# A graph attention layer's aggregation: three source tiles in split F32R products, their low parts made by transfers, a ring of five logit buffers

## The reference, cut to what matters

```python
h = (x @ W.T).reshape(n, heads, out_ch)
a_src = jnp.einsum('nhc,hc->nh', h, att_src)
a_dst = jnp.einsum('nhc,hc->nh', h, att_dst)
e = jax.nn.leaky_relu(a_src[src] + a_dst[dst], NEG_SLOPE)
m = jax.ops.segment_max(e, dst, num_segments=n)
ex = jnp.exp(e - m[dst])
denom = jax.ops.segment_sum(ex, dst, num_segments=n)
out = segment_sum(ex / (denom[dst] + EPS) * h[src], dst)   # 8 heads of 128, then + bias, relu
```

## Time and profile before

| what | value |
|---|---|
| median of three runs | 714.68 us (713.36 to 715.59) |
| the profiled execution's own time | 713.25 us |
| its span | 711.4 us |
| TensorE, VectorE, ScalarE, POOL busy | 701.1, 529.0, 420.0, 114.1 us |
| F32 products with PT (L1426) | 161.0 us, 730 records |
| transposes of L (L1402) | 94.2 us, 800 records |
| L2078 and L2087 on VectorE | 117.9 and 113.4 us, 80 each |

### The profile page before, as it was taken

How to read it: one execution, slowest core, us unless ns; L and a number is a source line. 1 busy time by engine, 2 the same in 40 slices (tenths; PEclk the granted TensorE clock), 3 DMA queues, 4 the chain that set the end, 5 groups by cost and what they waited for, 6 DMA issues and landing times.

```text
span 711.4 us, 13502 instructions
## 1 busy us (share of the span) xinstructions
PE 701.1 (99%) x4670; PEld 657.9 (92%) x4670; DVE 529.0 (74%) x878; ACT 420.0 (59%) x863; POOL 114.1 (16%) x95
## 2 busy tenths in 40 slices
PE   8899999999999999999999999999999999999997
PEld 6699999889899999999999999999999899999997
DVE  5999888698899999999999664445568752737232
ACT  4665584388688888888888754454443333522202
POOL 2559421000000000000000000000223331222202
PEclk9999999999999999999999999999999999999999
DMA  8727888645314131322310443201881734315102
GB/s 279 223 68 195 262 244 232 174 140 163 95 40 114 31 102 55 94 67 64 102 32 22 109 111 67 62 0 36 247 282 49 222 91 189 100 58 177 44 23 67
DMA packets 53362, 84.10 MB, mean 118 GB/s; under 512 B 15081, under 2 KB 36399, under 8 KB 53312
## 3 DMA queue, kind: packets, MB, share of 16 engines
q1 hardware_dynamic: 47628, 65.69, 32.6%
q10 hardware_dynamic: 4500, 13.82, 6.0%
q0 software_dynamic: 1184, 3.92, 1.9%
HBM read 68.09 MB, written 15.33 MB: 117 GB/s over the span
## 4 chain that ended last, share of the span: by engine, by line
PE 91%; DMA 4%; DVE 3%; issue 0%; POOL 0%; ACT 0%; ACTq 0%; SPq 0%; DVEq 0%
PE bank L1426 22%; PE bank L1571 13%; PE bank L1402 12%; PE bank L1498 12%; PE bank L1298 11%; PE bank L1675 4%; DMA w1n_sb<-in_W 3%; PE bank L1647 3%; PE bank L1213 3%; PE bank L1552 2%; PE bank L1701 1%; DVE x2f L2312 1%; PE bank L1215 1%; PE bank L1228 1%; PE bank L1732 1%; DVE fc_lo L2279 1%
## 5 line engine op out<-in xcount | busy, mean ns | idle before, releaser
L1426 PE MATMUL bank<-PT,h1s 125*128 125x250 f32 x730 | 161.0, 374 | 0.0
L1426 PEld LDWEIGHTS bank<-PT,h1s 125*128 125x128 f32 x730 | 135.3, 190 | 14.4
L2078 DVE SCALAR_TENSOR_TENSOR L<-asb,nadh 125x1250 f32<-125x1250 f32 x80 | 117.9, 1515 | 1.9 <-PE bank L1402 0.9
L2087 DVE CUSTOM_DVE_ANT_0 L<-L,LC 125x1250 f32<-125x1250 f32 x80 | 113.4, 1454 | 0.6 <-DMA LC<-log_count_scratch 0.4
L914 ACT ACTIVATE L<-L,nm 125x1250 f32<-125x1250 f32 x80 | 108.4, 1384 | 2.7 <-DVE nm L2087 1.9
L932 ACT COPY PT<-bank 125x500 f32<-125x500 f32 x165 | 87.4, 613 | 35.9 <-PE bank L1402 35.9
L1402 PE MATMUL bank<-ident,L 125*125 125x125 f32 x800 | 94.2, 273 | 0.0
L1402 PEld LDWEIGHTS bank<-ident,L 125*125 125x125 f32 x800 | 91.2, 189 | 0.9 <-issue 0.4
L1884 DVE TENSOR_TENSOR hotr<-iota,r 125x1500 f16<-125x1500 f16 x50 | 46.5, 931 | 7.8 <-PE bank L1215 4.2
L743 POOL MEMSET pick<- 128x90 f32 x1 | 0.2, 168 | 267.2 <-ACT hT L965 267.2
L1571 PE MATMUL bank<-h_hi,PT_hi 125*125 125x384 f32 x200 | 41.5, 350 | 0.0
(11 more groups left out here) (285 smaller groups left out, 1353.9 us busy)
## 6 DMA issues: line engine op xcount, KB each, us to landing
asb<-src_logit_rows SPq DMA_DIRECT2D x28, 312.5 KB, 3.9
atom_w<-in_atom_inT SPq DMA_DIRECT2D x5, 1152.0 KB, 12.5
atom_w<-in_atom_outT SPq DMA_DIRECT2D x5, 1152.0 KB, 9.4
log_count_scratch<-LCw SPq DMA_DIRECT2D x10, 546.9 KB
LC<-log_count_scratch SPq DMA_DIRECT2D x10, 546.9 KB
LCt<-log_count_scratch SPq DMA_DIRECT2D x10, 546.9 KB
h_scratch<-h1st ACTq DMA_DIRECT2D x10, 448.0 KB
rdT<-reciprocal_scratch SPq DMA_DIRECT2D x8, 500.0 KB, 4.6
```

The source lines that it names most:

```text
L1426: mm = pe.matmul(sums, h1s[q][:, s, :], PT[p][:, s, :], start=(s == 0), stop=(plain and s == NT - 1))
L2078: dve.scalar_tensor_tensor(L[r][:, :], asb[q][0:NP, 1, :], nadh[q][:, t:t + 1], asb[q][0:NP, 0, :], ALU.add, ALU.max).then_inc(stt_done, 1)
L2087: dve.tensor_tensor_reduce(out=L[r][:, :], in0=L[r][:, :], in1=LC[:, t, :], scale=-1.0, scalar=-FLOOR, op0=ALU.add, op1=ALU.min, accum_out ...
```

## The change

Tiles s = 0, 1, 2 of the sources go as split F32R products in heads 1 to 7, not tile 2 alone. ScalarE evicts, with signs, so that a sum of two stored tiles is the low part: PT_hi[0:2] as they are, PT[1] negated; PT[2:4] as they are, PT_hi[2] negated. VectorE still makes the low part of one tile, now s = 0. For s = 1 and 2 POOL (`lower_by_sum`) copies the raw PT[1:3] to PT_sum by a DMA, waits for it, and adds PT_hi[1:3] in a second, accumulating DMA. POOL also makes the features' low parts and their negatives once a head, for VectorE's one subtraction before. TensorE multiplies seven F32R products in `aggregate` and the two on PT_sum in `moved_parts`, one step later, between the fourth and the fifth bank of that step's transposes; the sums leave after it (`sums_done`). In ScalarE's step the exponential of the even tile comes ahead of the evictions.

L becomes a ring of five, and VectorE's list is shifted by a tile: in step k it makes tiles 2k+1 and 2k+2 (`blocks`; at a pair's border one, then three). It reads nad1 directly, and the nadh copy goes. asb comes in three pieces (PIECES), W2 in one load before the loop behind the wait for wattp; the W2 x att products stand in steps 3 and 4, wrow2 has another place in SBUF, and rdA lies where asb[1] was, so that its loads wait for the last logits. rrow holds one batch and its next copy waits for the store. Names of some semaphores change (t5_full is tb_full, t5_high is tb_evac).

```diff
@@ -61,8 +61,10 @@
 FLOOR = -1e29
 LATE = 6
 BATCHES = 3 * H // 2
-QUARTERS = 4
-PART = 2
+TURNED_BANKS = NG * NG * H
+PIECES = [0, 834, 1667, 2500]
+RING = 5
+PART = 0
 FIRST = 8 * NP
...
@@ -123,6 +125,25 @@
     if k == 2 * NG:
         return 3 * hh + 2, 2 * hh + 1, 1, LATE, NT
     return None
+def blocks(k, first):
+    if first and k < 3:
+        return [(2 * k, 2 * k + 1)]
+    if first and k == 3:
+        return [(6,), (7, 8)]
+    if k == 0:
+        return [(0,), (1, 2)]
+    if k == 2 * NG - 1:
+        return [(2 * k + 1,)]
+    return [(2 * k + 1, 2 * k + 2)]
+def moved(hh, kk):
+    return 16 * NG * hh + 16 * (kk // 2 - (NG // 2 - kk % 2))
...
@@ -736,6 +765,35 @@
                     start_out(n - 1)
                 if n + 1 < NT:
                     add_bias(n + 1)
+            def lower_by_sum(hh, kk):
+                n, p = 2 * NG * hh + kk, kk % 2
+                pool.wait_ge(tb_evac, NG * n + 2)
+                if not isinstance(n, int) or n > NG + 1:
+                    pool.wait_ge(sums_done, n + -(NG + 1))
+                alone(pool)
+                pool.dma_start(PT_sum[p][:, :, :].bitcast(F32), PT[p][:, 1:3, :]).then_inc(raw_moved, 16)
+                pool.wait_ge(raw_moved, 16 * n + (16 - 16 * NG))
+                alone(pool)
+                pool.dma_start(PT_sum[p][:, :, :].bitcast(F32), PT_hi[p][:, 1:3, :].bitcast(F32), accum_op=ALU.add
+                               ).then_inc(lower_moved[p], 16)
+                if kk % NG == 0:
+                    q = kk // NG % 2
+                    pool.wait_ge(features_high, 2 * hh + kk // NG)
+                    alone(pool)
+                    pool.tensor_tensor(h1p_lo[q][:, 0:2, :], h1s[q][:, 0:2, :], h1p_hi[q][:, 0:2, :].bitcast(F32),
+                                       ALU.subtract)
+                    pool.tensor_tensor(h1p_lo[q][:, 2, :], h1p_hi[q][:, 2, :].bitcast(F32), h1s[q][:, 2, :],
+                                       ALU.subtract)
+                    pool.tensor_scalar(h1p_neg[q][:, :, :], h1p_hi[q][:, 1:3, :].bitcast(F32), -1.0, None, ALU.mult
+                                       ).then_inc(features_lower, 1)
+            for kk in range(NG, 2 * NG):
+                lower_by_sum(0, kk)
+            with pool.Fori(1, H // 2) as hh:
+                for kk in range(2 * NG):
+                    lower_by_sum(hh, kk)
...
@@ -904,16 +962,16 @@
                 if i == NT - 2:
                     act.activation(early_exp[:, :], tiny[:, :], ACT.Exp)
-            def exp(hh, k, first=False, last=False):
+            def exp(hh, k, j, first=False, last=False):
                 if last:
                     return
                 q, g, n, h = at(hh, k, 0)
-                for j in range(2):
-                    r, t = (2 * k + j) % 4, 2 * g + j
-                    act.wait_ge(max_done, 2 * n + (j + 1))
-                    e = act.activation(L[r][:, :], L[r][:, :], ACT.Exp, bias=nm[q][:, t:t + 1], scale=-1.0,
-                                       accum_out=den[q][:, t:t + 1])
-                e.then_inc(exp_done, 1)
+                r, t = (2 * k + j) % RING, 2 * g + j
+                act.wait_ge(max_done, 2 * n + (j + 1))
+                e = act.activation(L[r][:, :], L[r][:, :], ACT.Exp, bias=nm[q][:, t:t + 1], scale=-1.0,
+                                   accum_out=den[q][:, t:t + 1])
+                if j == 1:
+                    e.then_inc(exp_done, 1)
             def evac(hh, k, first=False, last=False):
                 lag = 1
@@ -924,10 +982,19 @@
                     act.wait_ge(tb_full, NG * n + b + 1)
                     if b == 0 and not (first and k - lag < 2):
                         act.wait_ge(agg_done, n + -1)
+                        if not (first and k - 3 < NG):
+                            act.wait_ge(lower_moved[(k - 3) % 2], moved(hh, k - 3))
                     turned = bank[turned_bank(first, k - lag, b)]
                     if b == PART // 2 and not (first and k - lag < NG):
-                        act.copy(PT_hi[(k - lag) % 2][:, :], turned[0:NP, 0:GW])
-                        act.copy(PT[(k - lag) % 2][:, PART + 1, :], turned[0:NP, GW:2 * GW]).then_inc(tb_evac, 1)
+                        act.copy(PT_hi[(k - lag) % 2][:, 0:2, :],
+                                 turned[0:NP, 0:2 * GW].rearrange("p (s n) -> p s n", s=2))
+                        act.activation(PT[(k - lag) % 2][:, 1, :], turned[0:NP, GW:2 * GW], ACT.Copy, scale=-1.0
+                                       ).then_inc(tb_evac, 1)
+                    elif b == 1 and not (first and k - lag < NG):
+                        act.copy(PT[(k - lag) % 2][:, 2:4, :],
+                                 turned[0:NP, 0:2 * GW].rearrange("p (s n) -> p s n", s=2))
+                        act.activation(PT_hi[(k - lag) % 2][:, 2, :], turned[0:NP, 0:GW], ACT.Copy, scale=-1.0
+                                       ).then_inc(tb_evac, 1)
                     else:
                         act.copy(PT[(k - lag) % 2][:, 2 * b:2 * b + 2, :],
                                  turned[0:NP, 0:2 * GW].rearrange("p (s n) -> p s n", s=2)).then_inc(tb_evac, 1)
...
@@ -961,17 +1026,21 @@
                     for p in range(2):
                         act.wait_ge(h1_stored[p], TWO * NG)
                     act.wait_ge(rows_stored, 32)
-                act.wait_ge(agg_done, n + 1)
+                if first and k - lag < NG:
+                    act.wait_ge(agg_done, n + 1)
+                else:
+                    act.wait_ge(sums_done, n + (1 - NG))
                 act.copy(hT[:, ds(h, 1), g * GW:(g + 1) * GW].rearrange("c h n -> c (h n)"),
                          bank[2 + (k - lag) % 2][:, 0:GW]).then_inc(agg_out, 1)
             def step(hh, k, **at_end):
                 ahead = at_end.get("first") and k in (1, 2)
+                exp(hh, k, 0, **at_end)
                 if ahead:
-                    exp(hh, k, **at_end)
+                    exp(hh, k, 1, **at_end)
                 evac(hh, k, **at_end)
                 if not ahead:
-                    exp(hh, k, **at_end)
+                    exp(hh, k, 1, **at_end)
                 part_higher(hh, k, **at_end)
                 rows_out_of(hh, k, **at_end)
                 sums_out(hh, k, **at_end)
...
@@ -1422,16 +1491,29 @@
                 for s in range(NT):
                     if first and k == lag and s == 8:
                         pe.wait_ge(head_in[q], TWO * (hh + 1))
-                    if plain or s != PART:
-                        mm = pe.matmul(sums, h1s[q][:, s, :], PT[p][:, s, :], start=(s == 0), stop=(plain and s == NT - 1))
+                    if plain or s > 2:
+                        mm = pe.matmul(sums, h1s[q][:, s, :], PT[p][:, s, :], start=(s == (0 if plain else 3)), stop=(plain and s == NT - 1))
                 if not plain:
                     if g == 0:
                         pe.wait_ge(features_lower, h)
                     pe.wait_ge(lower_done, n + (1 - NG))
-                    pe.matmul(sums, h1p[q][:, 0, :], PT_hi[p][:, :], start=False, stop=False)
-                    pe.matmul(sums, h1p[q][:, 1, :], PT_hi[p][:, :], start=False, stop=False)
-                    mm = pe.matmul(sums, h1p[q][:, 0, :], PT_lo[p][:, :], start=False, stop=True)
+                    for s in range(3):
+                        high = h1p_neg[q][:, 1, :] if s == 2 else h1p_hi[q][:, s, :]
+                        pe.matmul(sums, high, PT_hi[p][:, s, :], start=False, stop=False)
+                        pe.matmul(sums, h1p_lo[q][:, s, :], PT_hi[p][:, s, :], start=False, stop=False)
+                    mm = pe.matmul(sums, h1p_hi[q][:, 0, :], PT_lo[p][:, :], start=False, stop=False)
                 mm.then_inc(agg_done, 1)
+            def moved_parts(hh, k, first=False, last=False):
+                lag = 3
+                if (first and k - lag < NG) or (last and k - lag >= 2 * NG):
+                    return
+                q, g, n, h = at(hh, k, lag)
+                p = (k - lag) % 2
+                sums = bank[2 + p][:, 0:GW]
+                pe.wait_ge(lower_moved[p], moved(hh, k - lag))
+                pe.matmul(sums, h1p_neg[q][:, 0, :], PT_sum[p][:, 0, :], start=False, stop=False)
+                pe.matmul(sums, h1p_hi[q][:, 2, :], PT_sum[p][:, 1, :], start=False, stop=True).then_inc(sums_done, 1)
             def turn_reciprocals(hh, k, first=False, last=False):
...
                     pe.wait_ge(watt_done, 6)
                 pe.transpose(bank[4][0:t1 - t0, 0:NP], rden[q][:, t0:t1], ident[0:NP, 0:NP]).then_inc(rden_turned, 1)
             def step(hh, k, **at_end):
-                for b in range(5):
+                for b in range(4):
                     turn_bank(hh, k, b, **at_end)
+                moved_parts(hh, k, **at_end)
+                turn_bank(hh, k, 4, **at_end)
                 turn_reciprocals(hh, k, **at_end)
                 aggregate(hh, k, **at_end)
...
@@ -2060,33 +2149,32 @@
                 if last:
```

(35 more changed lines are left out.)

145 lines of the change are left out of this document (75 added, 70 removed).

## The result

The changed kernel takes 729.41 us (median of four runs, 726.3 to 731.4) against 714.13 us of the kernel before on the same chip: a ratio of 1.0208 (1.0187 to 1.0229). It is slower by some 15 us, where 712.4 was forecast and the range ended at 721.0. The profiled execution took 726.3 us, with a span of 724.5 us against 711.4.

A forecast was written before the change was run, and what follows sets the result against it. TensorE, busy 99%, was taken as the bound, with VectorE hardly freer. TensorE -5.1, VectorE and POOL +2.5, the end +0.4 made -2.2 us: 712.4 us against the median of 714.68, range 709.0 to 721.0.

The forecast's parts named there:

- TensorE's part: TensorE's step in heads 1 to 7: fewer F32 products make it 6.19 us, a gain of 5.1 us in all.
- its 2.5: Loss of 2.5 us over six heads, as VectorE falls 0.8 us a head short once its lead is spent.
- ScalarE: ScalarE's step in the loop: 5.87 us, some 0.1 more with larger copies, staying 0.2 us under TensorE's 6.19.
- VectorE and POOL: In the loop, POOL's three operations cost VectorE 1.3 us a head, so it needs 31.9 us against TensorE's 31.1.
- The transfers: POOL's two DMAs per unit in the loop: 7.4 to 9.2 us together, hidden, at no cost; POOL keeps up.
- The room of 10.9 us for a unit's pair: Time from a unit's banks being out to ScalarE's evictions two steps on, in which both its DMAs must land.
- the 3.6 us of the earlier trace: Issue to landing of POOL's 336 KB loads, the nearest row used to estimate each of POOL's two DMAs.
- Rival C: POOL's transfers bound the loop and make it slower: 720 us with 11.4 us a pair; chance 0.21.
- C: Time of a unit's two POOL DMAs, one after the other: 7.4, 9.2 or 11.4 us; taken as 7.4 to 9.2.
- Its sign of recognition: In the loop, a wait of ScalarE's evictions on a DMA would show that the transfers bound it.
- Start and end: W2's one load before the loop costs nothing; unit 39's transfers at the end cost 0 to 1 us, taken as 0.4.

The follow-up runs named there:

- e2: Changed kernel with POOL's three feature operations between the raw transfer's issue and the wait for its landing; 720.0 us.
- e5: As e2, with the last unit (39) summed whole in F32 and no transfer for it; 716.9 us.
- e3: Changed kernel with the feature operations ahead of the unit's two transfers and, from head 2 on, 2 columns of each tile instead of 128; 725.6 us.
- e1: Changed kernel with POOL's three feature operations moved ahead of the unit's two transfers, once a head; 724.8 us.
- e9: As e5, with W2 loaded in eight pieces of 384 KB, one a head, instead of one load; 723.8 us.
- e10: As e9, with unit 38's two moved products between the sixth and seventh product of unit 39's F32 sum; 720.4 us.
- e11: As e5, with three idle POOL operations of 128 columns behind the accumulating transfer of each head's first three units; 757.3 us.
- e4: Changed kernel with both transfers of a unit moving 16 of 125 partitions from head 2 on; 716.1 us.
- e8: Changed kernel with the raw transfer issued from ScalarE's queue and the last unit summed whole in F32 without a transfer; 754.3 us.
- e12: As e5, with unit 38's two moved products between the sixth and seventh product of unit 39's F32 sum; 715.2 us.

## Why the prediction was wrong

- **TensorE's part: right.** The undisturbed step is 6.19 to 6.20 us as forecast, nine F32R products still take 0.117 us each, and where POOL is out of the way (e2, e5) 32 steps take 201.6 and 201.1 us. The forecast's terms for those steps give 203.95 - 32 x 0.147 + 2.5 = 201.7. That this fits so well is partly luck, as its 2.5 stands on a price for VectorE that was twice the measured one.
- **ScalarE: right.** It never set the pace; its waits for the first bank are smaller, not gone (10 us in 215 to 395 us).
- **VectorE and POOL: the mechanism was there, its price half.** VectorE loses 0.6 us a head (e2 against e3), not 1.3; with it VectorE needs 31.2 us against 31.1. What they cost POOL, 2.3 to 5.1 us a head in the changed kernel, was allowed for with the 3 to 4 us between its turns of 5 and of 8 to 9 us, though by the earlier trace rows it was read off as "0.6 us" of waiting, in proportion to a single long operation; here each of three short ones can pay such a wait.
- **The transfers: this is the step that failed, in the sentence "POOL's own turn (two issues, one landing, some 5 us; 8 to 9 where the three operations stand) keeps up".** The room of 10.9 us for a unit's pair was worked out with care, and a pair mostly stayed within it. But the turn of 8 to 9 us was compared with nothing: nobody was named who waits for POOL's third operation. TensorE does, at `features_lower`, in the first unit of each head, and its room is 8.7 to 9.0 us from the raw issue, so that even the forecast's own 8 to 9 us left less than 1 us, or nothing. It measured 9.2 to 11.8 us at five borders of heads. TensorE waited 6.8 us there. The five steps with these waits and the slow step behind the longest are 9.6 us longer than the same steps of e2, of 9.7 for the whole loop. The raw flight was 3.9 to 5.6 us at these borders rather than the 3.6 us of the earlier trace rows, with the accumulating transfer before it and SP's loads under way beside it; that row is of another kind of load, into a tile from memory, in a later stage. (Two of those 3.6 are 7.2 us, not the 7.4 of the text; nothing hangs on it.)
- **The queue's load, five turns and the operations in the 31 us of a head, was not added up either.** By the forecast's own figures it is 4 x 5 + 8.5 = 28.5 us, 2.5 us under. Measured it is 26.5 to 34.8, in the worst head 6.86, 5.73, 6.17 and 6.23 us and the turn with the operations 9.82. This made the wait at 262.52 some 0.8 us longer. In e1, where the queue is full, it goes with the 2.6 us by which the loop is longer than e2's.
- **Rival C** had the right place, POOL's transfers, and the right side, but not the mechanism. It let the pair's latency decide from C = 10.8 us; what decided was the latency of the raw transfer and the three operations, at a C of 9.6 to 10.0 where TensorE waited longest. Its sign of recognition, ScalarE's evictions waiting for a DMA, is small (4.8 us in four waits), and TensorE's wait for POOL was not on the list.
- **Start and end: wrong.** The end costs 4.0 us, not 0.4. C there is 11.3 us in place of 7.4 to 9.2 (raw 5.1, accumulating 6.2, beside rdA's and rdT's loads), and unit 39's raw transfer starts only when unit 38's raw one has landed. For the start 0 was taken, and 1.7 us were lost. 0.95 us of it are there before the first turn of the layer (148.86 against 147.91) and 0.74 of these at the products that wait for their weights at 29.24 us (28.50 before). The rest lies in the steps up to the sixth. W2's load was suspected and is not the cause (e9, e10); what is stays open. It varies from 1.3 to 5.2 us over these kernels.
- **The clock was left out.** The wait of 2.89 us was followed by a granted clock of 0.64 and 0.51 over four microseconds, and the next step took 1.6 us more than the usual 6.2; behind the four waits of up to 1.80 us the next step was as usual. In this kernel a wait can cost more than its length.

The Trainium skill (DMA: Bandwidth & Descriptors, Anatomy of one DMA — SWDGE (gpsimd) path) makes 2.6 us of such a transfer, as the prediction estimated from it. The trace comes near it only where nothing else is under way: 2.8 us for the raw transfer. The accumulating one takes 4.0 us alone, and among other transfers the medians are 4.3 and 4.2 us. The measurement decides. On descriptors that starve while VectorE holds the port (SBUF — State Buffer, Who interferes with whom) no run here gives an answer: the issues of the accumulating transfer keep to 0.83 to 0.95 us in the changed kernel, but the landings aren't split by what VectorE does.

## What to carry to other kernels

Name the consumer of every operation that a queue gets, and set the whole way to it against the time at which it is wanted. Here the way to POOL's third operation was a DMA's flight and three operations, and it was never compared with TensorE's step, while the way to the transfer itself was. Moving the operations ahead of the transfers gave back 7.1 us of the loop. Then cost a queue that issues a DMA and waits for its landing as if the flight were work: add the turns over one period, with every other operation in that queue, and compare the sum with the pace. Other work of such a queue is cheapest between the issue and the wait; that gave back another 2.6 us. And take the flight's time from a place where the neighbours fly as well: 2.8 us alone were 5.6 us at the border of two heads.

## What the runs showed of the hardware that was not expected

- A POOL operation beside VectorE's operations with two SBUF inputs often lasts until VectorE's ends, whatever its width: 1.18 to 1.43 us for 2 columns a tile at one border of e3, 1.5 us in the mean for 128 x 128 with one input (e11, shortest 0.52). Beside VectorE's low part, with one input in a bank, three operations of 2 columns took 0.9 us together. VectorE pays by width: nothing at 2 columns, 0.6 us a head at 640. The Trainium skill (SBUF — State Buffer, Who interferes with whom) says that a VectorE instruction with two SBUF inputs contends with a POOL one that reads SBUF; the rows agree, and add that what POOL pays there doesn't go by its width.
- An accumulating transfer of 244 KB from SBUF to SBUF takes 4.0 us alone (e11), the plain one 2.8; at 31 KB it is 2.4 against 1.8 (e4). Among other transfers the difference is gone, 4.2 against 4.3 us, as the plain one mostly flies beside the accumulating one issued just before it.
- The same transfer is slower from ScalarE's hardware queue than from POOL's: 5.0 us against 3.4 from its issue to POOL's next, with nothing else under way (e8).
- 384 KB a head more on the DMA engines (their busy share from 200 to 395 us is 0.66 instead of 0.61 or 0.62) made the loop 5.8 us longer (e9 against e5) and 4.2 us (e10 against e12), where a chain of small transfers was close to the bound.
